# The gates of the first 13 batches as sums of products on VectorE instead of matrix products on TensorE, and the rows' moments one step later

## The reference

```python
x = x + tanh(g_xattn[0]) * xattn(ctx, layernorm(x), ...)
#   q = ln @ Wq + bq;  k, v = split(concat([xn, ln]) @ Wkv + bkv)
#   out = softmax(q k^T * 128 ** -0.5) v @ Wo + bo          8 heads
x = x + tanh(g_ffn[0]) * ffn(layernorm(x), ...)
#   gates = (x @ Wg + bg) / (1 + 1e-6)                      256 -> 8
#   weights, indices = top_k(gates, 2);  weights = softmax(weights)
#   h = silu(x @ W1[e] + b1[e]);  out = sum over the two of weights * (h @ W2[e] + b2[e])
```

## Time and profile before

| | |
|---|---|
| median of 3 runs | 1516.0 us |
| the profiled execution | 1522.6 us, span 1520.9 us |
| PE busy | 1489.1 us, 98% |
| DVE busy | 1164.1 us, 77% |
| ACT busy | 950.5 us, 62% |
| POOL busy | 581.8 us, 38% |
| granted TensorE clock | 0.995 of full speed |

### The profile page before, as it was taken

One profiled execution on the slowest core, in us unless ns is written; L12 is line 12 of the kernel. 1 busy time (PEld: TensorE's weight loads), 2 busy tenths in 40 slices (PEclk: granted clock), 3 DMA queues, 4 the chain that ended last, 5 costly groups with the idle time before them and its releaser, 6 DMA issues. The chain is left out here.

```text
span 1520.9 us, 29833 instructions
## 1 busy us (share of the span) xinstructions
PE 1489.1 (98%) x10326; PEld 1369.7 (90%) x10326; DVE 1164.1 (77%) x2753; ACT 950.5 (62%) x2058; POOL 581.8 (38%) x650
## 2 busy tenths in 40 slices
PE   8999999999999999999999999999899999999997
PEld 7889888898888888898888988888899999999996
DVE  7878787878878787877878778787767776666685
ACT  5665656656555565556655565655668877777775
POOL 4323423333342332433333342332545445554542
PEclk9999999999999999999999999999999999999999
DMA  6010102101010110101011010012656654555463
GB/s 196 29 36 22 48 10 49 37 21 43 22 49 8 49 43 22 36 22 50 12 46 43 22 47 11 8 44 75 150 128 174 182 145 127 131 137 152 126 182 77
DMA packets 70576, 106.92 MB, mean 70 GB/s; under 512 B 11513, under 2 KB 55606, under 8 KB 70302
## 3 DMA queue, kind: packets, MB, share of 16 engines
q1 hardware_dynamic: 54462, 85.98, 17.2%
q0 software_dynamic: 15824, 18.98, 7.8%
q10 hardware_dynamic: 144, 0.05, 0.0%
HBM read 86.64 MB, written 18.35 MB: 69 GB/s over the span
## 5 line engine op out<-in xcount | busy, mean ns | idle before, releaser
L942 POOL TENSOR_SCALAR probs<-probs,rsum 128x512 f32<-128x512 f32 x256 | 176.9, 704 | 590.7 <-DVE rsum L1639 590.0
L1162 ACT ACTIVATE pt_hi<-turn 128x512 fp32r<-128x512 f32 x256 | 139.1, 595 | 233.2 <-PE turn L1318 231.7
L968 POOL DMA_INDIRECT out_rows<-yo,token x71 | 127.0, 1789 | 188.3 <-DVE yo L1815 170.0
L1764 DVE TENSOR_TENSOR ht_lo<-hs,ht_hi 128x512 fp32r<-128x512 f32 x142 | 98.1, 691 | 117.6 <-ACT ht_hi L1129 113.1
L1061 ACT ACTIVATE probs<-score,nbias 128x512 f32<-128x512 f32 x256 | 173.2, 686 | 1.9 <-DVE nbias L1635 1.8
L1120 ACT ACTIVATE hs<-ph,vecs 128x256 f32<-128x256 f32 (+1 forms) x284 | 114.4, 458 | 95.5 <-PE ph L195 89.1
L1633 DVE TENSOR_REDUCE smax<-score 128x1 f32<-128x512 f32 x256 | 167.8, 682 | 7.7 <-PE score L195 7.4
L1891 DVE TENSOR_TENSOR pt_lo<-turn,pt_hi 128x512 fp32r<-128x512 f32 x256 | 164.2, 683 | 8.6 <-ACT pt_hi L1162 8.4
L193 PE MATMUL py<-w_hi,ht_lo 128*128 (+1 forms) x568 | 162.8, 287 | 3.0 <-DVE ht_lo L1764 2.2
L195 PE MATMUL py<-w_hi,ht_hi 128*128 (+1 forms) x568 | 160.8, 283 | 0.0
L194 PE MATMUL py<-w_lo,ht_hi 128*128 (+1 forms) x568 | 160.8, 283 | 0.0
(11 more groups left out here) (246 smaller groups left out, 4720.2 us busy)
## 6 DMA issues: line engine op xcount, KB each, us to landing
w_raw<-in_L_ffn_W SPq DMA_DIRECT2D x45, 1024.0 KB, 5.3
spread<-mean_and_factor SPq DMA_DIRECT2D x15, 512.0 KB, 3.6
xhat_rows<-rows SPq DMA_DIRECT2D x16, 264.0 KB, 2.2
x_raw<-in_x SPq DMA_DIRECT2D x16, 256.0 KB, 3.0
c_raw<-in_ctx SPq DMA_DIRECT2D x16, 256.0 KB, 3.3
out_rows<-x SPq DMA_DIRECT2D x16, 256.0 KB, 2.3
z_turned<-in_x_turned SPq DMA_DIRECT2D x15, 256.0 KB, 3.8
z_turned<-in_ctx_turned SPq DMA_DIRECT2D x15, 256.0 KB, 4.3
```

What stands on the lines that cost most here:

```text
L942: last = pool.tensor_scalar(probs[n % 2][:, t, :], probs[n % 2][:, t, :], rsum[:, n % 2, t:t + 1], 1.0, ALU.mult, ALU.mult)
L968: pool.indirect_dma_start(out=A["out"], out_offset=bass.IndirectOffsetOnAxis(ap=token[:, u:u + 1].bitcast(U32), axis=0), in_=yo_of(t)[:, s ...
L1162: act.activation(pt[0][:, 2 * t:2 * t + 2, :], turn[t][:, :].rearrange("p (j i) -> p j i", j=2), ACT.Copy).then_inc(s_pthi, 1)
L1764: dve.tensor_tensor(lo[:, :], hs[n % N_HS][:, :], hi[:, :].bitcast(F32), ALU.subtract).then_inc(s_hlo, 1)
```

## The change

For batches 0 to 12 (DOT_B = 13) the units t and g and the copy to `x2t` are gone. `gates` is made by DVE: for each of the 8 experts and 2 halves of the rows one instruction multiplies 256 columns of `rows` with the expert's column of `Wg`, which lies on every partition in the new tensor `wg_wide`, and sums them into one column of `gates`. These 16 products lie in three steps: at h = 3 three behind `kt_lo` and one behind `v_lo`; at h = 4 and at h = 5 one ahead of `kt_lo`, three behind it, one behind `v_lo` and one behind `ot_lo`. largest(), choose(), unit r and weigh() come a step later (h = 5, 6, 7), find_places() and list_tokens() at h = 0 of the next batch. The bias is added by an instruction of its own. For all batches the moments of `x2` move from the end of h = 1 to behind `kt_lo` of h = 2, and norm_rows() from h = 1 to h = 2. The last three batches keep units t and g. SP loads `wg_wide` (1 MB) from a new input, the transpose of `Wg`.

```diff
+DOT_B = EARLY_B - 1
...
-        if h == T_STEP and 1 <= b < B:
+        if h == T_STEP and DOT_B < b < B:
             units.append(("t", b - 1))
-        if h == G_STEP and 1 <= b < B:
+        if h == G_STEP and DOT_B < b < B:
             units.append(("g", b - 1))
-        if h == W_STEP and 1 <= b < B:
+        if h == (W_STEP if b > DOT_B else W_STEP + 1) and 1 <= b < B:
             units.append(("r", b - 1))
...
+            weights_split(sp, "o1")
+            sp.dma_start(wg_wide[:, :, :].rearrange("p e d -> p (e d)"),
+                         A["gate_rows"].rearrange("e d -> (e d)").partition_broadcast(P)).then_inc(s_wg_wide, 16)
...
-                if h == R_STEP and 1 <= b < B:
+                if h == R_STEP + 1 and 1 <= b < B:
                     norm_rows(b - 1)
...
-                if h == L_STEP and 1 <= b < B:
+                if h == L_STEP and DOT_B < b < B:
                     list_tokens(b - 1)
+                if h == 0 and 2 <= b < DOT_B + 2:
+                    list_tokens(b - 2)
...
+            def dots(b, first, end):
+
+                dve.wait_ge(s_xn, b + 1)
+                dve.wait_ge(s_wg_wide, 16)
+                own.wait()
+                for q in range(first, end):
+                    e, t = divmod(q, TT)
+                    own.mark(dve.scalar_tensor_tensor(out=dot_junk[:, q % 4, :], in0=rows[b % 2][:, t, 0:D], scalar=1.0,
+                                                      in1=wg_wide[:, e, :], op0=ALU.mult, op1=ALU.mult,
+                                                      accum_out=gates[:, t, e:e + 1]))
+
             def largest(b):
 
-                dve.wait_ge(s_read, read_number["g", b] + 1)
+                if b < DOT_B:
+                    own.wait()
+                    own.mark(dve.tensor_tensor(gates[:, :, :], gates[:, :, :],
+                                               bg[:, :].unsqueeze(1).to_broadcast([P, TT, E]), ALU.add))
+                    own.wait()
+                else:
+                    dve.wait_ge(s_read, read_number["g", b] + 1)
...
+            def x2_moments(b):
                 dve.wait_ge(s_x2, b + 1)
                 moments("c", [x2[b % 2][:, t, :] for t in range(TT)], mv_c, s_mvc, s_xn, b)
...
+                summed = 1 <= b <= DOT_B
+                if summed and h == G_STEP:
+                    dots(b - 1, 4, 5)
+                if summed and h == G_STEP + 1:
+                    dots(b - 1, 10, 11)
...
+                        if h == R_STEP + 1 and 1 <= b < B:
+                            x2_moments(b - 1)
+                        if summed and h == T_STEP:
+                            dots(b - 1, 0, 3)
+                        if summed and h == G_STEP:
+                            dots(b - 1, 5, 8)
+                        if summed and h == G_STEP + 1:
+                            dots(b - 1, 11, 14)
...
-                        if h == at and i != STEPS - 1:
+                        if h == at + (summed and at >= G_STEP) and i != STEPS - 1:
                             part(b - 1)
+                if h == 0 and 2 <= b < DOT_B + 2:
+                    find_places(b - 2)
```

More of the change, by code:

```diff
@@ L444, in layer @@
         spread = sb("spread", [P, P, 2, JT])
+        wg_wide = sb("wg_wide", [P, E, D])
+        dot_junk = sb("dot_junk", [P, 4, D])
         x2, rows = [x2_0, x2_1], [rows0, rows1]
@@ L529, in layer @@
         s_padz, s_chosen, s_place, s_routing = sem("padding_zero"), sem("chosen"), sem("places"), sem("routing_consts")
+        s_wg_wide = sem("gate_weights_wide_in")
         s_dve, s_pool = sem("dve_self"), sem("pool_self")
@@ L1196, in _ @@
                     act.activation(tgate[:, :], gate[:, :], ACT.Tanh).then_inc(s_tg, 1)
-                if i % H == E_STEP and 1 <= i // H < B:
+                if i % H == (E_STEP if i // H > DOT_B else E_STEP + 1) and 1 <= i // H < B:
                     exp_gap(i // H - 1)
@@ L1920, in _ @@
                 for u in steps[i]:
+                    if u[0] == "o" and summed and h == T_STEP:
+                        dots(b - 1, 3, 4)
+                    if u[0] == "o" and summed and h == G_STEP:
+                        dots(b - 1, 8, 9)
+                    if u[0] == "o" and summed and h == G_STEP + 1:
+                        dots(b - 1, 14, 15)
                     if u[0] in "vogr":
                         read_unit(*u)
+                if summed and h == G_STEP:
+                    dots(b - 1, 9, 10)
+                if summed and h == G_STEP + 1:
+                    dots(b - 1, 15, 16)
                 if i == 0:
@@ L1953, in _ @@
             residual(B - 1)
+            x2_moments(B - 1)
             dve.wait_ge(s_mvc, B)
@@ L2040 @@
         aps[name] = nc.dram_tensor("in_" + name, (B, D, T), F32, kind="ExternalInput").ap()
+    arrays["in_gate_rows"] = np.ascontiguousarray(np.asarray(inputs["L0_ffn_Wg"]).T)
+    aps["gate_rows"] = nc.dram_tensor("in_gate_rows", (E, D), F32, kind="ExternalInput").ap()
     aps["out"] = nc.dram_tensor("out_rows", (TOKENS + P, D), F32, kind="ExternalOutput").ap()
```

## The result

The changed kernel takes 1537.35 us (median of four runs, 1535.42 to 1543.0); beside it the kernel before took 1515.74 (1515.47 to 1516.01). The ratio is 1.0145, 95% interval 1.013 to 1.016. The prediction was 1507, with 1490 to 1532 as its range. The profiled execution of the changed kernel took 1535.69, with a span of 1533.9 and a granted clock of 0.988 of full speed (before: 0.995).

What follows compares the result with a forecast made beforehand. PE, busy 98% of the span, and its waits for DVE were taken as the bound. 0.65 us a batch, 8.5 over 13, plus 1.1 for two more h = 2 steps gave 9.6 off: 1507 us, range 1490 to 1532.

Steps and rivals of the forecast that it cites:

- Moments moved: In h = 2, moments behind `kt_lo` let `smax` start earlier, removing PE's wait of 0.57 us in 15 steps.
- Transposes and gate products gone: On PE, 0.47 + 0.92 = 1.39 us of work removed in each of 13 batches, 18.1 us if nothing else becomes late.
- A product's cost: On DVE, 0.43 us from one 256-column product to the next, 16 a batch; bounds 0.35 and 0.50.
- The lock in h = 4: DVE's products and POOL's CAST and `kvt_lo` wait for each other's shared SBUF ports; the step takes 9.15 us.
- the walk: Step-by-step schedule of h = 3 to h = 6 with products at 0.43 us, giving 1507 us; chance 0.46.
- 1 (no collision): In h = 4 POOL's long instruction lets small reads through, so products don't wait: 1491 us; chance 0.13.
- 2 (POOL keeps both halves): POOL holds the ports through both normalisation halves, so product 4 starts at 7.0 instead of 6.3: 1530 us; chance 0.22.
- 3 (half rate, 0.68): DVE's products run at half rate, 0.68 us each, making waits in h = 4 to 6: 1558 us; chance 0.07.
- the prediction's lower bound for full rate: On DVE, 0.35 us from one product to the next, with the accumulator read hidden.
- the rule on two sources: On DVE, the skill's statement that two SBUF sources that aren't bf16 halve this operation's throughput; refuted only without accumulator.
- 4 (some tenths more at `kt_lo`): A few tenths more at `kt_lo` of h = 4 or 5, margin 0.1: nothing gained, 1516 us; chance 0.12.
- POOL's four list DMAs move a step, between two normalisations as now: On POOL, the DMAs writing the lists move a step later, with no cost counted.

Runs made afterwards that it cites:

- experiment 3: The kernel before with only the moments of the residual's sum and norm_rows moved from h = 1 to h = 2: 1510.4 us, ratio 0.9948.
- Experiment 5: The changed kernel with lists in h = 5 and the products laid out anew, none around `kt_lo` of h = 4: ratio 0.986.
- experiment 1: The changed kernel with the lists of the first 13 batches written in h = 5 instead of h = 0: 1501.3 us.
- 2: The kernel before with only the lists moved, from h = 7 to h = 0 of the next batch: 1540.7 us.
- experiment 12: The kernel before with only the lists written in two halves, in h = 0 and h = 5 of the next batch: ratio 0.998.
- experiment 8: The changed kernel with lists in h = 5 and moments and norm_rows back in h = 1: 1517.3 us beside 1521.6 for the kernel before.
- 10: The changed kernel with lists in h = 5 and four extra indirect DMAs in h = 0, their words 64 bytes apart: 1513.2 us.
- 11: The changed kernel, lists in h = 5, extra h = 0 words 512 bytes apart: some 10 us more than experiment 1 would take on that chip.
- 7: The changed kernel with lists in h = 5 and four extra indirect DMAs in h = 0, their words side by side: 1594.8 us.
- 6: The changed kernel with two of the four list DMAs left in h = 0 and two moved to h = 5: ratio 0.989.
- 9: The changed kernel with lists halved between h = 0 and h = 5 and no products around `kt_lo` of h = 4: 1496.3 us, ratio 0.983.

## Why the prediction was wrong

- **Moments moved (0.57 in 15 steps): right.** h = 2 takes 7.90, and the edit alone is worth 7.9 us by the ratio, 6.5 by the medians (experiment 3), where 15 x 0.57 = 8.5 were said.
- **Transposes and gate products gone (1.39 a batch): right.** h = 3 is 7.90 wherever x is in time.
- **A product's cost: 0.43 taken, 0.345 measured.** With POOL out of the way they start at 184.48, 184.82, 185.17 in the changed kernel:

```profile
184.48 0.41 DVE L1567 SCALAR_TENSOR_TENSOR dot_junk<-rows,wg_wide 128x256 f32<-128x256 f32 x1
184.82 0.08 DVE L1567 DVE_READ_ACCUMULATOR dot_junk<-rows,wg_wide 128x1 f32 x1
184.82 0.42 DVE L1567 SCALAR_TENSOR_TENSOR dot_junk<-rows,wg_wide 128x256 f32<-128x256 f32 x1
```

- **The lock in h = 4: right in kind, 9.15 said and 8.70 measured.** One product of 1.96 behind `kvt_lo`, as the walk had it; with the cheaper products PE's wait for `qt_lo` is 0.3 instead of 1.05, while the wait for the normalisation is 0.5 instead of 0.2. Experiment 5 shows that the 0.8 us are these products' place; that the cheaper product makes up the difference of 0.45 is argued from its price.
- **Rivals.** 1 (no collision) is refuted by the 1.96. 2 (POOL keeps both halves) is refuted by the product behind `v_lo`, 0.56 us at 738.28 in the step of experiment 5, with POOL's two halves running from 737.88. 3 (half rate, 0.68) is refuted by the 0.345, which is the prediction's lower bound for full rate. So the rule on two sources in the Trainium skill, Vector Engine (DVE) Microarchitecture Reference, Points that are easy to get wrong, does not hold for this form either. 4 (some tenths more at `kt_lo`) did not occur: the changed kernel's waits for `kt_lo` in h = 4 are none in a clean batch. No rival was about the loads, so the range had no room for them.
- **"POOL's four list DMAs move a step, between two normalisations as now", costed at nothing: this is the step that failed.** It looked at POOL's time, where they are indeed free, and not at what they do to the queue that comes next. Before, their last issue ended 10.4 us ahead of SP's store and loads; now 2.5 us. That is 36 us of the result: experiment 1 takes them away with one line, and 2 puts 24 us on the kernel before with another, 16 of them by the same wait. Without it the prediction's own sum nearly comes out, 1501.3 measured against 1507. The 5.7 between them are about the step of h = 4 (13 x 0.45 = 5.9).

What the prediction's profile had to say on it: x landed 7.2 us behind its issue in batch 2, 5.4 in batch 3 and 3 to 4 us in the others, and nobody waited for it. A load that is late in a few batches and waited for in none is a margin that shrinks somewhere, and it was not asked what set it. The step of h = 2 of batch 2, 10.11 instead of 8.47, was to be seen too; it was ScalarE's stand of experiment 12.

Open: why the harm falls from batch 2 to batch 8 and comes back at 12; why 256 words do nothing and 512 do so much, and how much of that is their distance; why close words hurt; and what ScalarE, PE and DVE lack in the odd single steps of experiments 1, 5, 8, 10 and 11.

## What to carry to other kernels

- A DMA that moves costs more than its issue: list which transfers come near its new place, on any queue, and what waits for them at once. Here four small DMAs 10.4 us ahead of the loads cost DVE no wait, and 2.5 us ahead they cost 36 us. The loads had one step to land, and the wait was on the engine that everything hangs on.
- Small writes to neighbouring words in DRAM, right ahead of loads, are worth keeping away from them. Cutting them in two helped here as well, and the test writes did no such harm at 64 bytes apart. Busy DMA engines at a few GB/s were their sign.
- A long step has the reason that its waits name. The late x was the natural suspect for the 10.11 us, and experiment 12 was expected to cure it; DVE's waits acquit it in one row.
- Where products wait for GpSimd's instructions, put them where its long one isn't: 13 x 0.75 us here for the order alone.

## What the runs showed of the hardware

- Four indirect DMAs of 128 words of 4 bytes each, the last one ending 2.5 us ahead of a store of 256 KB and four loads of as much, made the loads take 14 to 15 us instead of 3 to 4. The median packet stayed at 46 ns, 74 of 1280 took 0.6 to 5.8 us.
- 13 batches of such DMAs to adjacent words cost 81.6 us more than the same ones to words 64 bytes apart (1594.8 against 1513.2).
- Behind four such DMAs in one go an engine at times stood in front of an instruction that had no condition or a fulfilled one: PE 2.7 us in experiment 8 and 6.1 in 7, ScalarE up to 9.4 in 7. With two and two (6, 9, 12) none did.
- A product of 256 columns with an accumulator and both inputs in SBUF follows the one ahead by 0.345 us: the read of the accumulator (0.08) is hidden. Behind GpSimd's `kvt_lo` of 2.46 us it took 1.96 instead of 0.41.
